# Background blocks one unit sooner, behind the second score of an even unit, with their rows added between two maxima steps

## The chip, the cores and the metric

The kernel runs on one core of a Trainium2 chip. The metric is the device time of one execution in microseconds. Five engines work side by side: TensorE (PE; its weight loads are shown as PEld), VectorE (DVE), ScalarE (ACT), GpSimd (POOL) and SyncE (SP), which here only issues transfers. Each takes its instructions from a queue of its own, and they wait for one another by semaphores.

## What is computed

A transformer layer with the norm behind each part, in float32: two sequences of 1024 rows with 512 features, grouped attention (32 query heads of 16, 8 key heads) with rotary angles, then a gated feed-forward part with 1408 inner features.

```python
Q, K = rope(x @ Wq.T + bq), rope(x @ Wk.T + bk)          # 32 and 8 heads of 16
V = x @ Wv.T + bv
w = softmax(einsum('bhqd,bhkd->bhqk', Q, repeat(K, 4)) / sqrt(16))
x = layernorm(x + (w @ repeat(V, 4)) @ Wo.T + bo)
g, u = (x @ gate_w.T) * gate_s, (x @ up_w.T) * up_s
x = layernorm(x + ((silu(g) * u) @ down_w.T) * down_s)
```

## The kernel before

**Units.** Attention is cut into 256 units: 16 pairs n of sequence and key head, with 16 units v each (two halves of the queries by 8 tiles of 128 keys). Code writes a unit as u = 16 n + v, or as the pair (n, v). PE does in each unit, by the loop that begins at L704: four scores (`scores`, L470, 512 queries by 128 keys for one query head g), each followed by one half step of maxima (`advance`, `maxima_half`, L448), and once the weighted sum of the unit before (`weigh`, L489): behind the last score in an even unit, behind the third in an odd one. A score tile stands in one of three PSUM banks, used in turn; the fourth score of an odd unit takes two of them, 128 columns and 384. ACT turns each into exponents (`exponent`, L784), which frees the bank.

**Maxima.** Softmax needs the largest score of each row before the scores are built. So PE computes the products of queries and keys twice: `maxima_half` runs 24 steps (12 units) ahead. A step has two halves, 512 keys each, in one of two slots of two banks. DVE reduces a step either whole (L991) or by halves (L987), alternately (`maximum`). A slot, or half slot, is free for PE once DVE has read it. When 16 steps are done, which is in units with u % 8 == 3, DVE joins the results (L1005). POOL splits them into a high and a low part in the same unit (`split_max`, L1316 and L1318). DVE transposes the parts behind its first step of the next unit (`turn_max`, L1021), and SP writes them to memory and reads them back into extra rows of the queries (`write_max`, L1564 and L1567) in units with u % 8 == 4. The scores of unit u % 8 == 0 that comes four units later need them.

**Background.** Eleven blocks of other work are set between the scores. Six project queries or keys for later (`project_at`: (n, v) to a job; 24 products of 512 columns, L387), one builds the values of the second sequence (`values_at`, products of 128 columns, L429), four make the attention's output rows (`out_at`, 24 products, L515). They stand in odd units, v = 3 or 11, behind the third score and ahead of the weighted sum. A block borrows two of the three score banks (`free_banks`), one half of the work in each.

A projected half is taken out by ACT (`evacuate_raw`, L770). Then SP swaps the halves of the rows by two transfers (`swap_halves`, L1530 and L1531), and POOL turns them by the angles in three passes over 1024 columns (`rope`, L1329, L1330, L1332). In later units ACT rounds each half and POOL takes the remainder (`low_half`, L1337), then SP writes both out; these steps are placed by `rope_end`. Values and output rows are added by DVE (`add_values`, L970; `add_rows`, L1057), and in the units of `norm_at` DVE also does the norm of the rows of the block before (`first_norm`, L1033 to L1041).

**Order.** All queues are written out by hand: each engine's program is one loop over the units with tests on (n, v). The order inside one unit of POOL's loop is, cut to three of its steps (L1464 to L1476):

```python
if u % 8 == 3 and apart(steps_done(u) // 16 - 1):
    split_max(steps_done(u) // 16 - 1)
if at_u in project_at:
    rope(project_at[at_u])
...
    elif what in ("h0", "h1"):
        low_half(j, int(what == "h1"))
```

Of the kernel before, what the change touches and what calls it, by code (L numbers as in the profile page):

```python
# [70 lines left out]
def post_ln_layer(nc, xT_d, x_d, wqk_d, wv_d, bqk_d, bv_d, wo_d, bo_d, wf_d, gs_d, us_d, ds_d,  # L71
# [6 lines left out]
    with ExitStack() as ctx:  # L78
# [123 lines left out]
        def bank(i):  # L202
            return PS2[:, i, :] if i < 3 else PV[:, :]
# [57 lines left out]
        stream = [(n, qt, g) for n in range(NG) for qh in range(2) for qt in range(4 * qh, 4 * qh + 4)  # L261
                  for g in (2, 0, 3, 1)]
        jobs = [(0, 1), (0, 2), (0, 3), (1, 4), (1, 0), (1, 1), (1, 2), (1, 3)]
        project_at = {(1, 11): 2, (4, 11): 3, (5, 3): 4, (6, 3): 5, (8, 3): 6, (8, 11): 7}
        rope_end = {(0, 1): (0, "h0"), (0, 2): (0, "h1"), (0, 3): (0, "out"),
                    (0, 4): (1, "rope"), (0, 8): (1, "h0"), (0, 10): (1, "h1"), (0, 11): (1, "out")}
        for at_u, j in project_at.items():
            u0 = 16 * at_u[0] + at_u[1] + 7
            rope_end.update({divmod(u0, 16): (j, "h0"), divmod(u0 + 2, 16): (j, "h1"), divmod(u0 + 3, 16): (j, "out")})
        values_at = (2, 11)  # L270
        out_at = {(10, 3): 0, (10, 11): 1, (11, 3): 2, (11, 11): 3}
        norm_at = {(10, 11): 0, (11, 3): 1, (11, 11): 2}
        recip_at = {(2, 13): 0, (4, 13): 1, (6, 5): 2, (8, 5): 3, (10, 5): 4, (12, 5): 5, (14, 5): 6}
        divide_at = {divmod(16 * n + v + 4, 16): kc for (n, v), kc in recip_at.items()}
        gather_at = {(n, {0: 13}.get(n, 5)): n + 2 for n in range(NG - 2)}
# [31 lines left out]
        score_bank = {}  # L307
# [13 lines left out]
            return c if p == len(pieces(c)) - 1 else (c, p)  # L321

        def free_banks(u):
            last = score_bank[4 * u + 2, 0]
            return (last + 1) % 3, last

        def ffn_slots(x):
# [34 lines left out]
        def tensor(e):  # L362
# [94 lines left out]
            def scores(u, g, p=0):  # L457
                n, v = divmod(u, 16)
                qh, kt = divmod(v, 8)
                c = 4 * u + g  # L460
                cols, i = pieces(c)[p], score_bank[c, p]
                clear(bank_free[i])
                w.wait_ge(*max_in[n % 3].at(2 * n + qh))
                if n == 0:
                    for point in first_rows[qh]:
                        w.wait_ge(*point)
                else:
                    w.wait_ge(*rows_in[n % 3].at(n))
                rows = slice(64 * (g // 2), 64 * (g // 2) + NC_ + 2)
                e.matmul(score_tile(i)[:, cols], Kt[n % 3][rows, 128 * kt:128 * kt + 128],  # L470
                         Qt[n % 3][rows, g % 2, 512 * qh + cols.start:512 * qh + cols.stop], start=True, stop=True).then_inc(
                    *pe_score.next(piece(c, p)))
                bank_free[i] = act_exp.at(piece(c, p))
# [216 lines left out]
            def background(u):  # L690
                at_u, pair = divmod(u, 16), free_banks(u)
                if at_u in project_at:
                    for h, i in enumerate(pair):
                        project_half(project_at[at_u], h, i, (0, 1, 2, 3))
                if at_u == values_at:
                    for t in range(8):
                        value_rows(1, t, pair[t // 4])
                if at_u in out_at:
                    t2 = out_at[at_u]
                    out_project(False, 0, t2, [bank(i) for i in pair], [bank_free[i] for i in pair])  # L700
                    for j, i in enumerate(pair):
                        bank_free[i] = dve_y.at((False, 0, 2 * t2 + j))

            for u in range(SPLIT):  # L704
                at_u = divmod(u, 16)
                for g in range(4):
                    scores(u, g)
                    advance(1)
                    if len(pieces(4 * u + g)) == 2:
                        scores(u, g, 1)  # L710
                    if u >= 1 and g == (3, 2)[u % 2]:
                        background(u)
                        weigh(u - 1)
                if at_u == (15, 1):
                    flag_sum()
                if at_u == (15, 2):
                    w.wait_ge(*dve_flag.at("flag"))
# [12 lines left out]
        def scalar(e):  # L730
# [188 lines left out]
            for u in range(SPLIT):  # L919
                at_u = divmod(u, 16)  # L920
                for g in range(4):
                    exponent(u, g)
                    if g == 2 and at_u in project_at:
                        for h, i in enumerate(free_banks(u)):
                            evacuate_raw(project_at[at_u], h, i)
                if u >= 1:
                    finish(u - 1)
                if at_u in rope_end and rope_end[at_u][1] in ("h0", "h1"):
                    round_half(rope_end[at_u][0], int(rope_end[at_u][1] == "h1"))
                if at_u == (15, 2):  # L930
                    w.wait_ge(*dve_flag.at("flag"))
# [11 lines left out]
        def vector(e):  # L943
# [22 lines left out]
            def add_values(b, h, i):  # L966
                w.wait_ge(*pe_val.at((b, h)))
                w.wait_ge(*landed["bv"].at())
                w.wait_ge(*pool_one.at())
                e.tensor_tensor(  # L970
                    Vp[:, b, 4 * h:4 * h + 4, :, 0:HD], bank(i).rearrange("p (t v c) -> p t v c", t=4, v=NKV),
                    bv[:, :].rearrange("p (o v c) -> p o v c", o=1, v=NKV).to_broadcast([128, 4, NKV, HD]),
                    ALU.add).then_inc(*dve_val.next((b, h)))

            def maximum(k, halves=(0, 1)):
                if k >= len(stream):
                    return
                s, hh = slot_of(k), k // 16
                g, qt = stream[k][2], stream[k][1]
                c0 = 4 * g + qt % 4  # L980
                if hh >= 2:
                    w.wait_ge(*low_max(hh - 2))
                if by_halves(k):
                    for h in halves:
                        w.wait_ge(*pe_max.at((k, 0) if h == 0 else k))
                        col = nmx[:, hh % 2, c0 + 16 * (h == 0):c0 + 16 * (h == 0) + 1]
                        e.tensor_reduce(col, slot_pair(s)[:, h, :], AX.X, ALU.max, negate=True).then_inc(  # L987
                            *dve_max[s].next((k, 0) if h == 0 else k))
                else:
                    w.wait_ge(*pe_max.at(k))  # L990
                    e.tensor_reduce(nmx[:, hh % 2, c0:c0 + 1], slot_pair(s), AX.XY, ALU.max, negate=True).then_inc(  # L991
                        *dve_max[s].next(k))
                if 1 in halves and k % 16 == 15:
                    join_max(hh)
                    if not apart(hh):
                        split_max(hh)
                        turn_max(hh)
                if k % 16 == 0 and k > 16 and apart(hh - 1):
                    turn_max(hh - 1)
# [48 lines left out]
            def first_norm(x, b, t2):  # L1048
                key = (x and b == 1, b, t2)
                measure_rows(rows_of(b, t2), [dve_y.at((x and b == 1, b, 2 * t2 + 1))], key)  # L1050
                scale_rows(rows_of(b, t2), key, dve_x1, key)
# [201 lines left out]
            for u in range(SPLIT):  # L1253
                at_u = divmod(u, 16)
                maximum(next(steps))
                k = next(steps)
                if at_u in norm_at or at_u in out_at or at_u == values_at:
                    maximum(k, (0,))
                    if at_u in norm_at:
                        first_norm(False, 0, norm_at[at_u])  # L1260
                    if at_u == values_at:
                        for h, i in enumerate(free_banks(u)):
                            add_values(1, h, i)
                    if at_u in out_at:
                        add_rows(False, 0, out_at[at_u], [bank(i) for i in free_banks(u)])
                    maximum(k, (1,))
                else:
                    maximum(k)
                if at_u in recip_at:
                    reciprocal(recip_at[at_u])  # L1270
                if at_u == (15, 0):
                    w.wait_ge(*pool_low.at((FI - 1, 2)))
                    e.tensor_reduce(lowb[:, :], lowsum, AX.X, ALU.max).then_inc(*dve_flag.next("max"))
                if at_u == (15, 1):
                    w.wait_ge(*pe_flag.at())
                    e.tensor_scalar(flag[0:1, 0:1], slot_pair(before_flag % 2)[0:1, 0, 0:1], 0.0, None,
                                    ALU.is_gt).then_inc(*dve_flag.next("flag"))
                if at_u == (15, 2):
                    w.wait_ge(*dve_flag.at("flag"))
# [559 lines left out]
```

## Time and profile before

| | us |
|---|---|
| median of 3 runs (lowest, highest) | 1038.73 (1037.86, 1039.15) |
| profiled execution | 1039.11 |
| its span, first to last instruction | 1037.2 |
| PE busy | 1017.1 |
| DVE busy | 794.2 |
| ACT busy | 664.9 |
| POOL busy | 278.6 |

The profiled execution lies 0.4 us above the median, and 1.9 us of it lie around the span. Busy times are shares of the whole span, of which attention takes about the first 755 us and the feed-forward part the rest; the change lies in attention alone. Busy PE time includes matmuls that overlap, so the share says that PE is hardly ever empty, not how fast it goes; that is read from the distance between like instructions.

### The profile page before, as it was taken

The numbers are of one execution on the slowest core, as the hardware profiler recorded it, in microseconds if no ns is written. First come the engines' busy times: TensorE is split into PE (matmuls) and PEld (weight loads), VectorE is DVE, ScalarE is ACT, GpSimd is POOL, SyncE is SP. The second block draws the span as 40 slices with busy tenths as digits, with TensorE's granted clock in tenths as the row PEclk, the third lists the DMA queues.
The fourth block names the chain that finished last, engine by engine and source line by source line (L and its number), as shares of the span: only waits on it lengthen the run. The fifth ranks groups of instructions, "written<-read, shape, count | busy, mean of one in ns | idle before, by whom it ended". The sixth has DMA issues, their size and how long they took to land.

```text
span 1037.2 us, 15698 instructions
## 1 busy us (share of the span) xinstructions
PE 1017.1 (98%) x5858; PEld 534.6 (52%) x5858; DVE 794.2 (77%) x1139; ACT 664.9 (64%) x1346; POOL 278.6 (27%) x287
## 2 busy tenths in 40 slices
PE   8999999999999999999999999999999999999996
PEld 3643344433444433443444433333348888888885
DVE  5899978899779799779898898899822566563535
ACT  2359977789778898779666687888872420222221
POOL 2742021152245532246310055444101001000002
PEclk9999999999999999999999999899999999999999
DMA  5273517233215522345140447431238311311011
GB/s 205 82 211 105 123 34 215 59 99 87 54 53 143 91 73 48 85 85 133 35 79 12 119 136 151 109 128 41 100 119 195 120 41 41 82 51 32 1 40 43
DMA packets 64433, 94.88 MB, mean 91 GB/s; under 512 B 37536, under 2 KB 37920, under 8 KB 62272
## 3 DMA queue, kind: packets, MB, share of 16 engines
q1 hardware_dynamic: 63776, 93.10, 34.4%
q8 instruction: 48, 0.79, 0.3%
q10 hardware_dynamic: 576, 0.72, 0.2%
q14 instruction: 33, 0.27, 0.1%
HBM read 53.95 MB, written 27.00 MB: 78 GB/s over the span
## 4 chain that ended last, share of the span: by engine, by line
PE 94%; DVE 3%; ACT 1%; DMA 1%; issue 0%; POOL 0%; SPq 0%; POOLq 0%; DVEq 0%
PE PS L470 29%; PE PV L489 24%; PE PSA L559 15%; PE PS L576 6%; PE PSA L448 5%; PE PS L387 4%; PE PS L515 2%; PE PSA L515 2%; PE PV L576 2%; PE PSA L387 1%; PE PS L429 1%; ACT Bn L784 1%; DVE nmx L991 1%; DVE nmx L987 1%; DMA mscr<-mrow 1%; DMA A<-in_wqk 0%
## 5 line engine op out<-in xcount | busy, mean ns | idle before, releaser
L784 ACT ACTIVATE Bn<-PS 128x512 f32<-128x512 f32 x1128 | 535.5, 559 | 97.9 <-PE PS L470 85.6
L448 PE MATMUL PSA<-Kt,Qt 48*128 48x512 f32 x1024 | 388.5, 461 | 1.2 <-DVE Kt L964 0.8
L470 PE MATMUL PS<-Qt,Kt 50*128 50x512 f32 x1128 | 385.8, 436 | 3.8 <-DMA Qt<-mscr 2.5
L987 DVE TENSOR_REDUCE nmx<-PSA 128x1 f32<-128x512 f32 x512 | 327.3, 679 | 39.7 <-PE PSA L448 39.7
L470 PEld LDWEIGHTS PS<-Qt,Kt 50*128 50x128 f32 x1128 | 183.4, 185 | 311.5 <-ACT Bn L784 284.3
L991 DVE TENSOR_REDUCE nmx<-PSA 128x1 f32<-128x1024 f32 x256 | 312.2, 1219 | 22.6 <-PE PSA L448 20.3
L489 PE MATMUL PV<-Bn 128*32 128x512 f32 x2048 | 274.6, 608 | 0.0
L448 PEld LDWEIGHTS PSA<-Kt,Qt 48*128 48x128 f32 x1024 | 176.3, 184 | 11.7 <-DVE nmx L987 3.3
L559 PE MATMUL PSA<-x1Th,wr 128*128 128x512 f32 x344 | 135.5, 394 | 0.0
L559 PE MATMUL PSA<-x1Tl,wr 128*128 128x512 f32 x344 | 134.5, 391 | 0.0
L820 ACT ACTIVATE sg<-PSA,gs 128x512 f32<-128x512 f32 x43 | 29.6, 690 | 128.1 <-PE PSA L559 128.1
L1089 DVE SCALAR_TENSOR_TENSOR sg<-PSA,us,sg 128x512 f32<-128x512 f32 x43 | 32.2, 749 | 93.1 <-ACT sg L820 93.1
L489 PEld LDWEIGHTS PV<-Bn 128*32 128x32 f32 x2048 | 40.6, 108 | 76.0 <-issue 65.3
L1316 POOL CAST msp<-nmx 128x16 fp32r<-128x16 f32 x30 | 5.9, 196 | 262.3 <-DVE nmx L1005 262.3
L559 PEld LDWEIGHTS PSA<-x1Th,wr 128*128 128x128 f32 x344 | 64.6, 188 | 17.9 <-issue 3.6
L559 PEld LDWEIGHTS PSA<-x1Tl,wr 128*128 128x128 f32 x344 | 64.7, 188 | 13.3
L1402 POOL TENSOR_SCALAR ve<-mv 128x2 f32<-128x2 f32 (+1 forms) x11 | 2.8, 258 | 247.1 <-DVE mv L1036 247.1
L833 ACT CAST hTh<-sg 128x512 fp32r<-128x512 f32 x38 | 23.6, 620 | 44.0 <-DVE sg L1089 36.8
L1109 DVE TENSOR_TENSOR hTl<-sg,hTh 128x512 fp32r<-128x512 f32 x38 | 26.3, 692 | 33.1 <-ACT hTh L833 33.0
L1381 POOL TENSOR_TENSOR Bn<-Bn 128x1024 f32<-128x1024 f32 x8 | 19.4, 2419 | 98.4 <-DMA Bn<-rscr 98.4
L576 PE MATMUL PS<-wr,hTh 128*128 128x512 f32 x114 | 44.7, 392 | 0.0
L576 PE MATMUL PS<-wr,hTl 128*128 128x512 f32 x114 | 44.5, 391 | 0.0
(170 smaller groups left out, 909.4 us busy)
## 6 DMA issues: line engine op xcount, KB each, us to landing
Qt<-pscr SPq DMA_DIRECT2D x90, 128.0 KB, 5.2
A<-in_wf SPq DMA_DIRECT2D x11, 768.0 KB, 7.1
wr<-A SPq DMA_DIRECT2D x33, 256.0 KB, 2.8
pscr<-A SPq DMA_DIRECT2D x16, 512.0 KB, 3.5
vscr<-Bn SPq DMA_DIRECT2D x32, 256.0 KB, 3.0
Kt<-pscr SPq DMA_DIRECT2D x90, 64.0 KB, 2.8
A<-A SPq DMA_DIRECT2D x16, 256.0 KB, 3.7
Bn<-vscr SPq DMA_DIRECT2D x8, 512.0 KB
```

Source lines behind the costliest of these rows:

```text
L387: op = e.matmul(ps, v, t, start=first and i == 0, stop=last and end)
L448: op = e.matmul(PSA[:, 2 * s + h, :], Qt[n % 3][p:p + NC_, g % 2, 128 * qt:128 * qt + 128], Kt[n % 3][p:p + NC_, 512 * h:512 * h + 512], s ...
L470: e.matmul(score_tile(i)[:, cols], Kt[n % 3][rows, 128 * kt:128 * kt + 128], Qt[n % 3][rows, g % 2, 512 * qh + cols.start:512 * qh + cols. ...
L489: op = e.matmul(PV[32 * g:32 * g + 32, :], Bn[:, o:o + 32], Pb[c % NP_], start=(kt == 0), stop=(kt == 7), tile_position=(0, 32 * g))
L515: op = e.matmul(ps, t_, v, start=(k == 0 and i == 0), stop=(k == KT - 1 and i == len(pairs) - 1))
L559: op = e.matmul(gate_bank(x, q, j), v, t, start=(k == 0 and m == 0), stop=(k == KT - 1 and m == (1 if x else 0)))
L576: op = e.matmul(bank(t), v, t_, start=(i == 0 and m == 0), stop=(i == FI - 1 and end))
L784: e.activation(Pb[c % NP_][:, cols], score_tile(score_bank[c, p])[:, cols], ACT.Exp, scale=0.25).then_inc(*act_exp.next(piece(c, p)))
L820: e.activation(sg[q % 2], gate_bank(x, q, 0), ACT.Silu, scale=gs[:, i:i + 1]).then_inc(*act_silu.next((x, q)))
L987: e.tensor_reduce(col, slot_pair(s)[:, h, :], AX.X, ALU.max, negate=True).then_inc(*dve_max[s].next((k, 0) if h == 0 else k))
L991: e.tensor_reduce(nmx[:, hh % 2, c0:c0 + 1], slot_pair(s), AX.XY, ALU.max, negate=True).then_inc(*dve_max[s].next(k))
L1089: e.scalar_tensor_tensor(out=out, in0=gate_bank(x, q, 1), scalar=us[:, i:i + 1], in1=sg[q % 2], op0=ALU.mult, op1=ALU.mult).then_inc(*dve_ ...
```

## The change

All eleven blocks stand one unit sooner (v = 2 or 10) and, inside the unit, behind the second score and its half step instead of behind the third. The banks they borrow are those that are free there. ACT takes the projected halves out behind the second exponent. DVE adds rows and values (and does the norm) between the unit's whole step and the one by halves, which is no longer split around them. The swap on SP and the rope on POOL, which go by the same dictionary, move one unit with the block; the steps of `rope_end` stay in their units. The number of instructions stays the same.

```diff
-        project_at = {(1, 11): 2, (4, 11): 3, (5, 3): 4, (6, 3): 5, (8, 3): 6, (8, 11): 7}
+        project_at = {(1, 10): 2, (4, 10): 3, (5, 2): 4, (6, 2): 5, (8, 2): 6, (8, 10): 7}
...
-            u0 = 16 * at_u[0] + at_u[1] + 7
+            u0 = 16 * at_u[0] + at_u[1] + 8
...
-        values_at = (2, 11)
-        out_at = {(10, 3): 0, (10, 11): 1, (11, 3): 2, (11, 11): 3}
-        norm_at = {(10, 11): 0, (11, 3): 1, (11, 11): 2}
+        values_at = (2, 10)
+        out_at = {(10, 2): 0, (10, 10): 1, (11, 2): 2, (11, 10): 3}
+        norm_at = {(10, 10): 0, (11, 2): 1, (11, 10): 2}
...
         def free_banks(u):
-            last = score_bank[4 * u + 2, 0]
+            last = score_bank[4 * u + 1, 0]
...
+                    if g == 1:
+                        background(u)
                     if u >= 1 and g == (3, 2)[u % 2]:
-                        background(u)
                         weigh(u - 1)
...
-                    if g == 2 and at_u in project_at:
+                    if g == 1 and at_u in project_at:
                         for h, i in enumerate(free_banks(u)):
                             evacuate_raw(project_at[at_u], h, i)
...
-                if at_u in norm_at or at_u in out_at or at_u == values_at:
-                    maximum(k, (0,))
-                    if at_u in norm_at:
-                        first_norm(False, 0, norm_at[at_u])
...
-                    maximum(k, (1,))
-                else:
-                    maximum(k)
+                if at_u in norm_at:
+                    first_norm(False, 0, norm_at[at_u])
...
+                maximum(k)
```

## Rows read from the trace of the kernel before

**Rows 1.** The page's table of engines: busy us, share of the span, instructions.

```profile
PE 1017.1 (98%) x5858; PEld 534.6 (52%) x5858; DVE 794.2 (77%) x1139; ACT 664.9 (64%) x1346; POOL 278.6 (27%) x287
```

**Rows 2.** Busy time of each engine in a quiet stretch; waits there (us, times, longest).

```profile
460.00:500.00 40.00, 40.00 (x272) 15.17 (x270) 38.86 (x54) 36.15 (x77) 26.50 (x23) 1.00 0.36 98
PEld PS L470 <- ACT Bn L784: 20.1, 40, 0.8
```

**Rows 3.** PE's timeline over two units: start, duration, engine, line, operation, tiles, shape, count.

```profile
475.88 1.07 PE L489 MATMUL PV<-Bn 128*32 128x512 f32 x8
...
478.00 0.49 PE L470 MATMUL PS<-Qt,Kt 50*128 50x512 f32 x1
...
478.92 1.07 PE L489 MATMUL PV<-Bn 128*32 128x512 f32 x8
...
480.48 0.39 PE L470 MATMUL PS<-Qt,Kt 50*128 50x512 f32 x1
...
480.81 1.07 PE L489 MATMUL PV<-Bn 128*32 128x512 f32 x8
```

**Rows 4.** PE's timeline around the projection in unit (8,3): first and last product, sums.

```profile
417.63 1.07 PE L489 MATMUL PV<-Bn 128*32 128x512 f32 x8
...
419.80 0.50 PE L387 MATMUL PS<-xh,wh 128*128 128x512 f32 x1 [0.22 <-ACT Bn L784]
...
425.16 0.39 PE L387 MATMUL PS<-xl,wh 128*128 128x512 f32 x1
425.48 1.07 PE L489 MATMUL PV<-Bn 128*32 128x512 f32 x8
```

**Rows 5.** ACT, DVE, POOL, SP behind that block; POOL's group of `low_half`, mean in ns.

```profile
425.59 0.69 ACT L770 ACTIVATE A<-PS,bqk 128x512 f32<-128x512 f32 x1 [2.04 <-PE PS L387]
...
429.03 0.20 DVE L1021 STREAM_TRANSPOSE mrow<-msp 128x32 f32<-128x32 f32 x1
429.16 1.24 DVE L987 TENSOR_REDUCE nmx<-PSA 128x1 f32<-128x512 f32 x2
...
428.05 0.20 POOL L1316 CAST msp<-nmx 128x16 fp32r<-128x16 f32 x1 [25.14 <-DVE nmx L1005]
428.32 0.22 POOL L1318 TENSOR_TENSOR msp<-nmx,msp 128x16 fp32r<-128x16 f32 x1
430.67 2.38 POOL L1329 TENSOR_TENSOR A<-A 128x1024 f32<-128x1024 f32 x1 [2.13 <-DMA A<-A]
...
435.46 2.39 POOL L1332 TENSOR_TENSOR A<-A 128x1024 f32<-128x1024 f32 x1
...
429.26 0.59 SPq L1564 DMA_DIRECT2D mscr<-mrow  x1
431.27 0.53 SPq L1567 DMA_DIRECT2D Qt<-mscr  x2
...
L1337 POOL TENSOR_TENSOR A<-A 128x512 f32<-128x512 f32 x16 | 20.5, 1283 | 34.3 <-ACT A L776 34.3
```

**Rows 6.** DVE's timeline in unit (10,11), a block with rows and norm.

```profile
537.85 1.28 DVE L1033 BATCH_NORM_STATS2 st<-x1a 128x6 f32<-128x512 f32 x2
...
541.50 0.68 DVE L1057 TENSOR_TENSOR x1a<-x1a,PS 128x512 f32<-128x512 f32 x1
```

**Rows 7.** SP and PE around 645 us; then busy times, clock (1.00 is full) and DMA.

```profile
637.27 0.56 SPq L1564 DMA_DIRECT2D mscr<-mrow  x1
645.38 0.56 SPq L1567 DMA_DIRECT2D Qt<-mscr  x2
...
643.25 1.07 PE L489 MATMUL PV<-Bn 128*32 128x512 f32 x8
...
647.33 0.47 PE L470 MATMUL PS<-Qt,Kt 50*128 50x512 f32 x1 [2.53 <-DMA Qt<-mscr]
...
656.79 0.64 PE L489 MATMUL PV<-Bn 128*32 128x512 f32 x4
...
648.20:655.00 6.80, 6.61 (x29) 2.01 (x29) 4.14 (x5) 3.87 (x8) 1.56 (x2) 0.50 0.52 166
```

More of the change, by code:

```diff
@@ L1256, in vector @@
                 k = next(steps)
-                if at_u in norm_at or at_u in out_at or at_u == values_at:
-                    maximum(k, (0,))
-                    if at_u in norm_at:
-                        first_norm(False, 0, norm_at[at_u])
[L1261 to L1265, printed above, removed]
-                    maximum(k, (1,))
-                else:
-                    maximum(k)
+                if at_u in norm_at:
+                    first_norm(False, 0, norm_at[at_u])
+                if at_u == values_at:
+                    for h, i in enumerate(free_banks(u)):
+                        add_values(1, h, i)
+                if at_u in out_at:
+                    add_rows(False, 0, out_at[at_u], [bank(i) for i in free_banks(u)])
+                maximum(k)
                 if at_u in recip_at:
```

## Prediction

> **What bounds the kernel now.** The table of engines comes first: TensorE (PE) is busy for 98% of the span, so the page names it as the bound [rows 1]. That figure counts overlapping, modelled matmul ends, so I went on to one quiet stretch. There VectorE (DVE) is busy 38.86 of 40 us and ScalarE (ACT) 36.15, and PE's weight loads for scores waited on ACT's exponents for 20.1 us [rows 2]. Three engines run in lockstep, and none has much slack. The third view, PE's timeline of two units, shows the beat. The weighted sums (L489) start at 475.88 in an odd unit, 478.92 in the even one, 480.81 in the next odd one [rows 3]: 3.04 us and 1.89 us, 4.93 for a pair. The reader should see why 3.04 is so long: the third score of the even unit starts at 478.00, 0.92 before the sum, whereas in the following unit the third score (480.48) stands 0.33 before its sum. The stretch up to 478.00 and behind it is paced by exponents.
>
> The fourth view is a block of background work as it lies now, in an odd unit [rows 4]. From the sum at 417.63 to the sum at 425.48 are 7.85 us where 1.89 would stand without the block, so it costs 5.96. Its 24 products start from 419.80 to 425.16; the first waited 0.22 us for an exponent. During it ACT and DVE run dry, and right behind it comes the weighted sum (0.99 us), in which ACT has nothing either.
>
> The fifth view is what the other engines do after this block [rows 5]. Call T the start of its last product (425.16). ACT empties the second bank from 425.59 to 426.28 (T+1.12). GpSimd (POOL) splits the finished maxima at 428.05 and 428.32, ready at 428.54 (0.49 in all). Only then does it start the rope, at 430.67 (T+5.51), released by the swap transfer, and ends it at 435.46 + 2.39 = 437.85 (T+12.7).
>
> **The change, part by part.**
>
> *The block's place.* Now PE goes from the second score of the even unit to the block, then to the third and fourth score, then to the sum. The first bank that the block takes is the one that the third score waited for, so it starts where that score starts now, 478.00 - 475.88 = 2.12 behind the odd sum [rows 3]. Then 5.36 for the products [rows 4], 0.32 to the next score (as 425.16 to 425.48), and 0.33 + 0.33 for two scores that no exponent holds up, since ACT has drained meanwhile. That gives 8.46 for what is 3.04 without the block: 5.42 instead of 5.96, a gain of 0.54; with 0.23 between the two scores it would be 0.64. I take 0.56. The 11 blocks (six projections, one of values, four of output rows) give 11 x 0.56 = 6.2 us. ACT's evacuation ends at T+1.12 and the next score that needs the bank comes behind the sum at T+1.97; this cover is 0.8 us thick.
>
> *VectorE.* The rows are added after the whole step and before both halves, instead of between the halves. In the three units that also normalise, statistics and scaling take 541.50 - 537.85 = 3.65 us [rows 6]. They begin 0.6 sooner than now and still end inside the 5.4 us of products, so the first row is added before PE wants the bank. Both halves come some 0.6 us later; the slot they hold is wanted at T+2.5 and the first of them is read by about T+1.7. I cost this at nothing. Were the cover gone, it would be one 0.68 us reduction in each of 5 blocks.
>
> *What moves with the six projections.* The same dictionary places the swap on SP's queue and the rope on POOL's. On SP nothing is passed: the maxima are written in the next but one unit, still behind the swap. On POOL two queued instructions are passed: the split of the maxima is issued in units with u % 8 == 3, before the rope in the same unit today. With the rope in u % 8 == 2 it stands ahead of that split. The split then waits for the rope, the rope for the swap, and the swap for the evacuation.
>
> Who waits for the split: DVE's transpose of the maxima, queued behind its first reduction of unit u % 8 == 4, and behind it every later reduction. The times follow from T. PE: sums at T+0.98 (even), +2.87 (odd), +5.91 (even), and the third product of maxima in the unit after would start at 2.87 + 3.04 + 1.56 = T+7.47. DVE would come to its transpose at about T+6.5. But POOL ends the rope at T+12.7, the split takes 0.49 more [rows 5], so T+13.2; transpose 0.13 to the next reduction, that one 0.68 to its end, and PE may refill the half slot at T+14.1. Stall of PE: 14.1 - 7.47 = 6.6 us. PE's lead of two slots is already in the 7.47. Six of them: 39.6 us. DVE works off its two waiting steps while PE restarts; I take 0 for it, at most 0.3 each.
>
> *Two collisions.* Units (5,2) and (8,10) are also those in which POOL rounds the first half of the job before (L1337, 1.28 us [rows 5]). It was ahead of the rope by one unit and now falls between rope and split: 2 x 1.3 = 2.7 us with its gap.
>
> *The clock.* PE stands idle for 6.3 us in each stall. The trace has one such case: a wait of 2.53 us before 647.33, and from 648.2 to 655.0 the granted clock is 0.50, which is 1.2 instead of 2.4 GHz [rows 7]. From the sum at 643.25 to the one at 656.79 are 13.54 us against 3.04 + 1.89 + 3.04 = 7.97, a loss of 5.6; the wait put off the first score by 2.7, so the slow clock cost 2.8. With longer idle I take the same 2.8 for each of the six, 16.8 us. It is bounded below by 0 (the clock stays up) and above by 4.2, half again as much, if the clock takes longer to come back.
>
> The Trainium skill, "TensorE: Matmul & The Clock Gate", Part 1, says that the array runs at 1.2 GHz by default when idle and is let up to 2.4 GHz by sustained work. The trace agrees, with the 0.50 behind 2.53 us of waiting. By that rule all six stalls end at the low clock; without it the sum is 16.8 us shorter.
>
> **Sum**, against the profiled execution (1039.1 us, of it 1037.2 span): -6.2 + 39.6 + 2.7 + 16.8 = +52.9, so 1092.0. The median of the runs shown is 0.4 lower, so 1091.6.
>
> **Rivals.**
>
> (1) *Stalls without the slow clock.* The trace shows one fall of the clock in the middle of the span, so one case carries the whole term. If a stall of this kind does not bring it on, 1091.6 - 16.8 = 1074.8.
>
> (2) *The maxima come too late for the scores as well.* Behind the transpose (T+13.3) SP writes the maxima, 2.0 us to the reads (429.26 to 431.27), and a read landed 1.95 us after its issue (645.38 [rows 7] to the score at 647.33). That is T+17.8 with the gaps; the first score that needs them comes at about T+20.7. So 2.9 us remain. Where weights were being loaded, the write took 645.38 - 637.27 = 8.1 us [rows 7]; 6.1 - 2.9 = 3.2 us more in each of six, 1091.6 + 19 = 1111. Against it: the weights are loaded only from unit (11,5) on.
>
> (3) *The other side: the split is not held by the rope.* If POOL could take the split, whose maxima are ready, ahead of the rope, or if swap and rope were done by T+6.0 rather than T+12.7, DVE would find the split ready at T+6.5. No stall then, no slow clock, and only the gain remains: 1038.7 - 6.2 = 1032.5. The point that decides is whether the split's low part is ready at T+6.5. Against it: the rope's three passes alone take 7.2 us from a start at T+5.5, and nothing in the change touches POOL's order.
>
> The Trainium skill, "PSUM — Partial Sum Buffer", section "Engine vs sequencer instructions", calls the queues of ScalarE, VectorE and GpSimdE "strict FIFO". By it rival 3 is out; no row here shows POOL passing anything, and none could show that it never does.
>
> **Chances.** Forecast 0.72 (1080 to 1101: six times the clock's 0.8 to 4.2 around it); rival 1 0.10; rival 2 or otherwise longer 0.10; rival 3 0.05; stalls much smaller than worked out 0.03, of which 0.02 within 0.2%. A measurement of this kernel can tell about 0.2% from no change. Faster 0.05, same 0.02, slower 0.93. The range takes in rival 1 and the upper bound of the clock: 1073 to 1103.
>
> **What the changed profile would show.** The block's price: sum to sum 8.4 to 8.5 us in ten blocks, followed by 1.89. The chain of steps: on POOL the split directly behind the rope's third pass, or behind L1337, and in the table of waits DVE's transpose waiting six times for the split, 5 to 7 us each. PE's loads for L448 then wait for DVE's half reduction for about as long. The granted clock falls to 0.50 six times in the first half of the span. The four blocks of output rows and the one of values show no stall, only 0.5 to 0.6 us less. I am wrong in the main if the transpose does not wait; wrong in size if rope or swap take another time, or the clock stays at 1.00.

## The result and the profile after

The changed kernel takes 1094.0 us in the median of 4 runs (1092.2 to 1096.6) against 1038.3 for the kernel before: a ratio of 1.0535, 95% interval 1.0518 to 1.0551. The profiled execution took 1096.6 us with a span of 1094.7, so it lies 2.6 above the median. Lines of code after the change are some numbers off those of before: the transpose is L1022, the half reductions L988, the split L1313 and L1315, the rope L1326, L1327 and L1329.

The page's table of engines, after, answers to [rows 1]: PE's busy time rose by 19 us and the others' hardly at all, so 39 of the 57.5 us by which the span grew are idle PE.

```profile
PE 1035.7 (95%) x5858; PEld 540.9 (49%) x5858; DVE 795.7 (73%) x1139; ACT 665.4 (61%) x1346; POOL 278.0 (25%) x287
```

The tables of waits of DVE and of PE, after (who <- for whom: us in total, times, longest). Neither line exists in the kernel before.

```profile
DVE mrow L1022 <- POOL msp L1315: 41.3, 6, 7.7
PE PSA L448 <- DVE nmx L988: 38.7, 6, 7.2
```

Six waits of the transpose for the split, six waits of PE for the half reduction behind it. Four times the transpose waited 6.5 us, twice 7.7. The first of them, in the timelines of PE, POOL and DVE behind the projection in (1,10), whose last product starts at 134.5:

```profile
137.43 1.06 PE L489 MATMUL PV<-Bn 128*32 128x512 f32 x8
...
140.47 1.07 PE L489 MATMUL PV<-Bn 128*32 128x512 f32 x8
...
142.04 0.39 PE L470 MATMUL PS<-Qt,Kt 50*128 50x512 f32 x1
148.47 0.79 PE L448 MATMUL PSA<-Kt,Qt 48*128 48x512 f32 x1 [6.04 <-DVE nmx L988]
149.19 1.93 PE L489 MATMUL PV<-Bn 128*32 128x512 f32 x8
...
140.05 2.39 POOL L1326 TENSOR_TENSOR A<-A 128x1024 f32<-128x1024 f32 x1 [24.74 <-DMA A<-A]
142.39 2.35 POOL L1327 TENSOR_TENSOR A<-A 128x1024 f32<-128x1024 f32 x1
144.82 2.34 POOL L1329 TENSOR_TENSOR A<-A 128x1024 f32<-128x1024 f32 x1
147.10 0.20 POOL L1313 CAST msp<-nmx 128x16 fp32r<-128x16 f32 x1
147.38 0.22 POOL L1315 TENSOR_TENSOR msp<-nmx,msp 128x16 fp32r<-128x16 f32 x1
...
139.94 1.22 DVE L992 TENSOR_REDUCE nmx<-PSA 128x1 f32<-128x1024 f32 x1
147.63 0.21 DVE L1022 STREAM_TRANSPOSE mrow<-msp 128x32 f32<-128x32 f32 x1 [6.47 <-POOL msp L1315]
147.77 1.25 DVE L988 TENSOR_REDUCE nmx<-PSA 128x1 f32<-128x512 f32 x2
```

Read it from the bottom up. DVE ends its first reduction of unit (1,12) at 141.1 and could transpose; the maxima were joined at 140.0. POOL takes the split only at 147.10, behind three passes that began at 140.05. PE's third score of the next unit starts at 142.04, and the half step of maxima that belongs to it at 148.47. Compare [rows 5], where the split stood 2.1 us ahead of the rope.

The third view is busy time and granted clock of three stretches there (us; busy PE, PEld, DVE, ACT, POOL with counts; clock; DMA share; GB/s):

```profile
142.40:148.50 6.10, 0.06 (x2) 0.03 (x1) 0.87 (x3) 1.17 (x3) 5.04 (x5) 0.69 0.00 0
148.50:155.00 6.50, 6.50 (x28) 2.24 (x28) 5.09 (x7) 2.74 (x6) 0.00 (x0) 0.50 0.04 9
155.00:160.00 5.00, 5.00 (x37) 1.81 (x33) 4.14 (x6) 3.99 (x9) 0.00 (x0) 1.00 0.00 0
```

While PE idles the clock falls to its lower level (0.50, 1.2 GHz) and stays there for 6.5 us of resumed work; the weighted sum takes 1.93 us instead of 1.07, as behind the wait of [rows 7].

**Where 57.5 us of span come from.** I compared the starts of like weighted sums in both traces. The start of a weighted sum is a good mark, since every unit has one. Nine of the eleven blocks became 0.45 to 0.56 us cheaper, together -4.8. The block in (6,2) became 0.4 dearer, that in (10,10) 2.7 with the unit behind it. The six stalls add 6.8 or 6.9 (four) and 8.0 (two), together 43.4. The four units behind each add 2.1 to 3.5, together 15.4. One microsecond is from the start of the program, ahead of any changed instruction, and about 0.6 is given back in small amounts.

Block (10,10) is the one thing of a new kind. POOL, DVE and PE there:

```profile
592.17 2.41 POOL L1378 TENSOR_TENSOR Bn<-Bn 128x1024 f32<-128x1024 f32 x1 [16.16 <-DMA Bn<-rscr]
594.55 0.24 POOL L1399 TENSOR_SCALAR ve<-mv 128x2 f32<-128x2 f32 x1
594.87 0.73 POOL L1401 TENSOR_TENSOR ve<-ve,half 128x2 f32<-128x2 f32 x1
595.63 1.00 DVE L1042 TENSOR_SCALAR x1a<-x1a,mv,ve 128x512 f32<-128x512 f32 x2 [2.96 <-POOL ve L1401]
596.55 1.28 DVE L1058 TENSOR_TENSOR x1a<-x1a,PS 128x512 f32<-128x512 f32 x2
597.29 0.50 PE L470 MATMUL PS<-Qt,Kt 50*128 50x512 f32 x1 [1.62 <-DVE x1a L1058]
```

A division (L1378) stands in unit (10,9) and now runs when the norm needs its spread (L1399 and L1401), which waits behind it. The norm ends late, the rows are added late, and the third score waits 1.62 us for its bank. The clock fell behind that wait too, for 3.4 us. In (6,2) PE's first product waited 0.9 us for a split of weights that POOL does behind ten microseconds of bias additions; the split ended at 361.05 and the product began at 361.20.

### The profile page after: what moved, and what is told of

Read it like the earlier page. It is cut to its first block, busy times and chain, and to the rows that moved or that the text cites. A ratio compares the mean times of both kernels' runs of the same rounds, so it can differ in the third digit from the quotient of the medians.

```text
span 1094.7 us, 15698 instructions
## 1 busy us (share of the span) xinstructions
PE 1035.7 (95%) x5858; PEld 540.9 (49%) x5858; DVE 795.7 (73%) x1139; ACT 665.4 (61%) x1346; POOL 278.0 (25%) x287
## 4 chain that ended last, share of the span: by engine, by line
PE 85%; POOL 5%; DMA 3%; DVE 3%; issue 2%; ACT 1%; SPq 0%; POOLq 0%; DVEq 0%
PE PS L470 24%; PE PV L489 21%; PE PSA L559 15%; PE PSA L448 6%; PE PS L576 6%; PE PS L387 4%; PE PSA L515 2%; DMA A<-A 2%; PE PV L576 2%; PE PS L515 2%; PE PSA L387 1%; POOL A L1326 1%; PE PS L429 1%; POOL A L1329 1%; POOL A L1327 1%
## 5 line engine op out<-in xcount | busy, mean ns | idle before, releaser
L448 PE MATMUL PSA<-Kt,Qt 48*128 48x512 f32 x1024 | 395.7, 472 | 40.0 <-DVE nmx L988 38.7
L988 DVE TENSOR_REDUCE nmx<-PSA 128x1 f32<-128x512 f32 x512 | 327.4, 679 | 38.8 <-PE PSA L448 38.8
L470 PEld LDWEIGHTS PS<-Qt,Kt 50*128 50x128 f32 x1128 | 186.7, 189 | 319.7 <-ACT Bn L785 273.0
L489 PE MATMUL PV<-Bn 128*32 128x512 f32 x2048 | 284.8, 629 | 0.0
L448 PEld LDWEIGHTS PSA<-Kt,Qt 48*128 48x128 f32 x1024 | 180.2, 189 | 52.9 <-DVE nmx L988 44.6
L1399 POOL TENSOR_SCALAR ve<-mv 128x2 f32<-128x2 f32 (+1 forms) x11 | 2.9, 260 | 238.5 <-DVE mv L1037 238.5
L1378 POOL TENSOR_TENSOR Bn<-Bn 128x1024 f32<-128x1024 f32 x8 | 19.4, 2427 | 128.4 <-DMA Bn<-rscr 128.4
L1313 POOL CAST msp<-nmx 128x16 fp32r<-128x16 f32 x30 | 5.9, 198 | 173.9 <-DVE nmx L1006 173.8
L1326 POOL TENSOR_TENSOR A<-A 128x1024 f32<-128x1024 f32 x8 | 19.1, 2385 | 111.9 <-DMA A<-A 111.2
```

Of the source, the lines that this page charges most:

```text
L448: op = e.matmul(PSA[:, 2 * s + h, :], Qt[n % 3][p:p + NC_, g % 2, 128 * qt:128 * qt + 128], Kt[n % 3][p:p + NC_, 512 * h:512 * h + 512], s ...
L489: op = e.matmul(PV[32 * g:32 * g + 32, :], Bn[:, o:o + 32], Pb[c % NP_], start=(kt == 0), stop=(kt == 7), tile_position=(0, 32 * g))
L1326: e.tensor_tensor(raw, raw, cosT, ALU.mult).then_inc(*pool_rope.next((j, "cos")))
```

## The experiments

**e1_rope_behind_split: POOL's rope alone put back.** Every block stays in its new place.

```diff
-                if at_u in project_at:
-                    rope(project_at[at_u])
+                if divmod(u - 1, 16) in project_at:
+                    rope(project_at[divmod(u - 1, 16)])
```

> The changed kernel with the rope of the six projections put back one unit on GpSimd alone, behind the split of the maxima; all blocks stay where the change put them. Theory (rope ahead of the split in GpSimd's queue): no wait of VectorE's transpose for the split, no fall of the clock behind it, so only the gain of place remains, about 0.53 us in each of 11 blocks, less what two single waits take (0.9 us in unit (6,2), 2.7 us in unit (10,10)): 1033 to 1036 us. Rival A (the loss comes from the block's new place, such as both half reductions coming later): 1085 us or more. Rival B (place gives nothing by itself): 1038 to 1039 us.

Measured: 1035.6 us against 1038.8, ratio 0.9964 (0.9951 to 0.9978). POOL's timeline has the split ahead again, and no wait of the transpose is left:

```profile
139.19 0.20 POOL L1313 CAST msp<-nmx 128x16 fp32r<-128x16 f32 x1 [24.77 <-DVE nmx L1006]
139.47 0.22 POOL L1315 TENSOR_TENSOR msp<-nmx,msp 128x16 fp32r<-128x16 f32 x1
139.65 2.39 POOL L1326 TENSOR_TENSOR A<-A 128x1024 f32<-128x1024 f32 x1
```

So the whole loss came with one call in POOL's queue, and the place of the blocks is a small gain. By the starts of the sums it is 0.44 to 0.59 us in nine blocks less 0.3 in (6,2) and 0.2 in (10,10), 4.2 us in all. The block in (10,10) has the same order as in the changed kernel, with the division ahead of the spread, but it cost much less here: the division began 1.4 us behind the block's first product instead of 2.3, PE waited less, and the clock stayed up.

```profile
PE PS L470 <- DVE x1a L1058: 0.7, 1, 0.7
```

So what that order costs hangs on when the division's data land. About 1.3 of the gain was lost again in this execution at the wait for the maxima that stands in [rows 7], which took 4.2 us here instead of 2.5.

**e2_before_rope_first: the same exchange in the kernel before.**

```diff
+                if at_u in project_at:
+                    rope(project_at[at_u])
                 if u % 8 == 3 and apart(steps_done(u) // 16 - 1):
                     split_max(steps_done(u) // 16 - 1)
-                if at_u in project_at:
-                    rope(project_at[at_u])
```

> The kernel before with one edit: in the units of the projections GpSimd does the rope ahead of the split of the maxima instead of behind it. Theory: the same stall, and a longer one, since the block stands one unit nearer to the transpose: PE's next half slot is wanted at T+4.9 instead of T+7.5 and comes free at about T+14.3, so 9.4 us and 2.5 us of slow clock in each of six, 71 us: about 1110 us. Rival A (the loss belongs to the new place): 1038 to 1040 us.

Measured: 1108.1 us, ratio 1.0676 (1.0652 to 1.0699). Each of the six stalls adds 9.34 to 9.42 us, where 9.4 was worked out. PE's table of waits:

```profile
PE PSA L448 <- DVE nmx L987: 51.4, 6, 8.6
```

This is the cleanest sign of the cause: nothing else moved, and the stall is longer by about the time that the block stands nearer to the transpose (2.5 us, where 2.6 was worked out).

**e3_two_passes: a shorter rope.** One of its three passes, the multiplication by the sines, is left out for the six projections, so the kernel computes something else; only its time is of use.

```diff
-                e.tensor_tensor(qrot, qrot, sinT, ALU.mult).then_inc(*pool_rope.next((j, "sin")))
-                w.wait_ge(*pool_rope.at((j, "sin")))
+                if j < 2:
+                    e.tensor_tensor(qrot, qrot, sinT, ALU.mult).then_inc(*pool_rope.next((j, "sin")))
+                w.wait_ge(*pool_rope.at((j, "sin" if j < 2 else "cos")))
```

> The changed kernel with the rope of the six projections cut from three passes over 1024 columns to two (the multiplication by the sines is left out, so part of the computation is missing). Theory: each stall becomes shorter by just one pass, 2.4 us, 14.3 us in all, and the clock still falls behind 3.7 us of idleness: 1079 to 1081 us. Rival C (VectorE waits for something else, the swap's transfer or the read-back of the maxima): 1092 to 1095 us.

Measured: 1079.1 us, ratio 1.0383 (1.0367 to 1.0400), 14.9 less than the changed kernel. The transpose's six waits, now 5.4 us at most:

```profile
DVE mrow L1022 <- POOL msp L1315: 27.5, 6, 5.4
```

41.3 - 27.5 = 13.8 us, 2.3 for each pass of 2.35 us left out. The rope's length goes into the stall one for one. The clock still fell behind the 3.7 us of idleness left in four of the stalls and the 4.9 in the two others.

**e4_filler: PE kept at work in the stall.** Products with zero weights (`zero`, set once at the start; `FILL` is 6) are added to the weighted sum's bank, so the sum is the same.

```diff
...
                     scores(u, g)
+                    if g == 2 and divmod(u - 3, 16) in project_at:
+                        w.wait_ge(*dve_const.at())
+                        for _ in range(FILL + (at_u in ((5, 5), (8, 13)))):
+                            e.matmul(PV[:, :], zero[:, :], Bn[:, vo:vo + 512], start=False, stop=False)
                     advance(1)
...
```

> The changed kernel with PE kept at work during each of the six stalls: six (seven in units (5,5) and (8,13)) products of zero weights, 0.86 us each, added to the weighted sum's bank, behind the third score and ahead of the half step of maxima that has to wait. Theory (idleness brings the clock down, which costs 2.1 to 3.5 us behind each stall): the granted clock stays at 1.00 there, the stalls keep their end, and about 15 us come back: 1077 to 1081 us. Rival D (the 2.1 to 3.5 us are VectorE and ScalarE catching up, not the clock): 1093 to 1096 us.

Measured: 1083.5 us, ratio 1.0434 (1.0418 to 1.0450), so 10.5 less than the changed kernel where 15 was expected; between the two profiled executions it is 13.8 of span. The transposes' waits stayed (42.4 us). Behind the first stall the clock stays up:

```profile
148.30:155.00 6.70, 6.70 (x46) 2.52 (x47) 6.63 (x9) 4.25 (x9) 0.00 (x0) 1.00 0.03 6
```

The four units behind each stall add -0.01 to 0.12 us in five cases instead of 2.1 to 3.5. In the sixth, behind block (5,2), the swap's transfer landed 1.0 us later than in the changed kernel and the rope with it, so the filler ran out early: PE idled 2.04 us ahead of 320.30, the clock was at 0.50 from 322.3 to 325.7, and 1.1 us were lost. The slow clock is the cause of what is lost behind the stalls. That cost differs between executions: behind the six stalls it was 15.4 us in the changed kernel, 13.8 in e6 and 12.9 in e5. That may be part of the 4 us between the changed kernel's runs, which was not measured. Why the medians differ by less than the profiled executions is not settled beyond that.

**e5_low_half_first: the two collisions.**

```diff
+                if at_u in project_at and at_u in rope_end:
+                    low_half(rope_end[at_u][0], 0)
                 if at_u in project_at:
                     rope(project_at[at_u])
...
-                    elif what in ("h0", "h1"):
+                    elif what in ("h0", "h1") and at_u not in project_at:
```

> The changed kernel with GpSimd's remainder of the first half (low_half) put ahead of the rope in units (5,2) and (8,10). Theory (what stands between rope and split lengthens the stall by its own length): the two long waits of the transpose shrink from about 8.0 to 6.85 us like the other four, since the remainder is done while GpSimd waits for the swap anyway; 2.3 us less in all, about 1092 us. Rival (these two stalls are longer for another reason, such as transfers): they stay at 8.0 us.

Measured: 1090.5 us, ratio 1.0502 (1.0485 to 1.0519). All six waits are now 6.46 to 6.49 us:

```profile
DVE mrow L1022 <- POOL msp L1315: 38.9, 6, 6.5
```

41.3 - 38.9 = 2.4 us, 1.2 for each; the rest of the 3.5 was not traced to anything.

**e6_divide_later: the norm in (10,10).**

```diff
+        divide_at[10, 11] = divide_at.pop((10, 9))
```

> The changed kernel with one division (L1378, 2.4 us) moved from unit (10,9) to unit (10,11) on GpSimd, so that it no longer stands ahead of the spread that VectorE's norm in block (10,10) waits for. Theory (norm late by that division, rows added late, score bank late): PE's 1.6 us gap before the third score of (10,10) and the fall of the clock behind it vanish, the sum-to-sum distance of that block falls from 9.1 to the 7.4 of the other blocks of rows, 2 to 3 us less in all, about 1091.5 us. Rival (the norm does not fit into the block's products once the rows are added ahead of both halves): the gap stays above 1 us.

Measured: 1091.5 us, ratio 1.0509 (1.0492 to 1.0526). PE's gap in (10,10) is gone, and so is the fall of the clock behind it; the block and the unit behind it lie 3.2 us lower by the starts of the sums. The spread now comes at once and no longer follows the division:

```profile
590.60 0.24 POOL L1400 TENSOR_SCALAR ve<-mv 128x2 f32<-128x2 f32 x1 [16.79 <-DVE mv L1038]
590.92 0.73 POOL L1402 TENSOR_TENSOR ve<-ve,half 128x2 f32<-128x2 f32 x1
...
599.11 2.39 POOL L1379 TENSOR_TENSOR Bn<-Bn 128x1024 f32<-128x1024 f32 x1
```

**e7_split_on_vector: the split taken from POOL's queue instead of the rope.** In the six half heads DVE splits the maxima itself.

```diff
+        own_split = [(16 * n + v + 1) // 8 + 1 for n, v in project_at]
         def apart(hh):
-            return 1 <= hh < 2 * NG - 1
+            return 1 <= hh < 2 * NG - 1 and hh not in own_split
```

> The changed kernel, GpSimd's rope still in the block's own unit, but in the six half heads concerned VectorE splits the maxima itself, as it does for the first and the last. Theory (only the split's place in GpSimd's queue links the rope to the scores): no stall and no slow clock, at a price of two short VectorE instructions in six units: 1034 to 1038 us. Rival (rope, swap or late read-back of the maxima hold PE up in another way as well): above 1050 us.

Measured: 1068.8 us, ratio 1.0278 (1.0258 to 1.0298). My theory was wrong here by more than 30 us, and the rival right: something else holds PE up. POOL, DVE and PE behind the first block:

```profile
139.73 2.36 POOL L1328 TENSOR_TENSOR A<-A 128x1024 f32<-128x1024 f32 x1 [24.73 <-DMA A<-A]
139.74 2.39 DVE L1015 CAST msp<-nmx 128x16 fp32r<-128x16 f32 x1
142.06 2.33 POOL L1329 TENSOR_TENSOR A<-A 128x1024 f32<-128x1024 f32 x1
142.16 2.27 DVE L1017 TENSOR_TENSOR msp<-nmx,msp 128x16 fp32r<-128x16 f32 x1
144.46 0.21 DVE L1024 STREAM_TRANSPOSE mrow<-msp 128x32 f32<-128x32 f32 x1
...
145.84 0.79 PE L450 MATMUL PSA<-Kt,Qt 48*128 48x512 f32 x1 [4.19 <-DVE nmx L994]
```

No semaphore is missing: DVE runs the two instructions of 16 columns, and each lasts until the POOL pass under way ends, 2.39 and 2.27 us where the same forms take 0.17. In three of the six units only the second waited. There the first had begun 0.01 to 0.02 us ahead of the pass, while in the other three it began as little behind it:

```profile
279.04 0.17 DVE L1015 CAST msp<-nmx 128x16 fp32r<-128x16 f32 x1
279.06 2.38 POOL L1328 TENSOR_TENSOR A<-A 128x1024 f32<-128x1024 f32 x1 [19.68 <-DMA A<-A]
```

PE idled 4.2 us where both waited and 1.9 where one did, and the clock fell behind five of the six.

**e9_vector_split_quarters: e7 with shorter POOL instructions.**

```diff
+                parts = [slice(256 * i, 256 * i + 256) for i in range(4)] if j >= 2 else [slice(0, 1024)]
-                e.tensor_tensor(raw, raw, cosT, ALU.mult).then_inc(*pool_rope.next((j, "cos")))
+                for c in parts:
+                    e.tensor_tensor(raw[:, c], raw[:, c], cosT[:, c], ALU.mult).then_inc(*pool_rope.next((j, "cos")))
...
```

> The kernel of e7 (VectorE splits the maxima itself in six half heads) with each pass of the six ropes cut on GpSimd into four instructions of 256 columns. In e7 VectorE's two instructions of 16 columns, 0.17 us elsewhere, took 2.2 to 2.4 us and ended together with a GpSimd pass over 1024 columns. Theory (two VectorE instructions whose operands lie in SBUF wait for the GpSimd instruction under way, to its end): with pieces of about 0.6 us each takes at most some 0.8 us, PE's gaps of 1.9 to 4.2 us shrink below 1 us, the clock stays up: 1036 to 1043 us. Rival (VectorE waits for the whole rope or for semaphores, whatever the length of a piece): as e7, 1065 to 1072 us.

Measured: 1040.8 us, ratio 1.0022 (1.0013 to 1.0032). DVE's second instruction, first in e7, then here (ns, least/median/most of 8):

```profile
L1017 DVE TENSOR_TENSOR msp<-nmx,msp x8: 174/2230/2266, 52.6 to 774.7; 128x16 fp32r<-128x16 f32 x8
```

```profile
L1017 DVE TENSOR_TENSOR msp<-nmx,msp x8: 174/590/655, 51.2 to 741.2; 128x16 fp32r<-128x16 f32 x8
```

The wait follows the length of the single POOL instruction, 2.35 us or 0.7. PE's waits for the half reduction sum to 2.1 us instead of 18.4, and the clock no longer falls behind them. That settles e7.

**e10_quarters: the control.** The same pieces in the changed kernel, split still on POOL.

> The changed kernel with each pass of the six ropes cut into four instructions of 256 columns, the split of the maxima still on GpSimd behind them: the control to e9. Theory (the queue's order alone makes the stall): the transpose still waits for the whole rope, which becomes a little longer by its nine further instructions: 1093 to 1098 us. Rival (it is the length of single GpSimd instructions that holds VectorE up in the changed kernel too): below 1080 us.

Measured: 1100.1 us, ratio 1.0587 (1.0569 to 1.0604), 2 us above what I gave. The pieces are less efficient than I took them for: three passes last 8.5 us instead of 7.1, and the waits grow from 41.3 to 49.2.

```profile
DVE mrow L1022 <- POOL msp L1315: 49.2, 6, 9.0
```

So in the changed kernel it is the order of the queue that counts, and the length of the single instruction only adds.

**e8_mended: what the runs point to.** e1 with three edits more.

```diff
+        divide_at[10, 11] = divide_at.pop((10, 9))
+        ffn_at[12, 13] = ffn_at.pop((12, 8)) + ffn_at[12, 13]
...
-                if at_u == (5, 12):
+                if at_u == (5, 13):
                     add_bo(0, u)
```

> The kernel of e1 with three further edits: the first addition of the output bias one unit later, behind the split of the weights that the block in (6,2) waits for; the division moved to (10,11) as in e6; one 768 KB weight load moved from unit (12,8) to (12,13), behind the write of the maxima that waits among such loads. Theory: the single gaps of 0.85 and 0.7 us go, and the gap of 4.2 us with its fall of the clock becomes shorter or goes, 2 to 5 us less than e1: 1030 to 1034 us. Rival: the gap before unit (13,0) comes from the reads of the keys and queries alone and stays; 1034 to 1036 us.

Measured: 1030.1 us, ratio 0.9921 (0.9906 to 0.9936), the fastest of all. All eleven blocks now gain 0.44 to 0.55 us, and the clock falls nowhere but at the end.

```profile
core 0: 1026.2 us, clock 0.998
```

**e11_before_load_later: how much of it is the block's place.** The weight load's edit alone, in the kernel before.

> The kernel before with the last edit of e8 alone: one 768 KB weight load moved from unit (12,8) to (12,13), behind the write of the maxima. In the trace of before, PE waited 2.53 us for the read-back and then ran 6.8 us at the low clock, 5.6 us in all. Theory (the write stands behind that load's packets, and the wait brings the clock down): the wait falls below 1 us, the clock stays at 1.00, 4 to 6 us less: 1033 to 1035 us, and the place of the blocks then accounts for about 4 to 5 us of the gain of e8. Rival (the packets of keys and queries ahead of it are what delays the write): within 1 us of before.

Measured: 1034.1 us, ratio 0.9963 (0.9951 to 0.9976). PE's wait for the read-back fell to 1.2 us, where I had said below 1, and the clock stayed at 1.00 from 640 to 660:

```profile
PE PS L471 <- DMA Qt<-mscr: 1.2, 1, 1.2
...
640.00:660.00 20.00, 18.58 (x128) 7.21 (x131) 18.23 (x27) 16.50 (x36) 10.66 (x15) 1.00 0.48 167
```

The write of the maxima was still slow: from its issue to the read-back's were 6.6 us instead of 8.1, against 2.0 in [rows 5]. So that load makes up a quarter of the delay, and the rival, which blamed the keys and queries, may be right about the rest; no run moved those. The wait shortened by 1.3 us, and most of the 4.1 us came from the clock that no longer fell.

So 4.1 of e8's 8.5 us go with that load, which has nothing to do with the change, and that leaves 4.4 for the place of the blocks with POOL's queue set right around it. By the starts of the sums in e8's profile the eleven blocks gain 5.8 us, and in that execution the wait for the read-back is gone altogether, so the split of the 8.5 is good to about a microsecond.

## Why the prediction held, point by point

The forecast was 1091.6 us; 1094.0 was measured, 2.4 above it. The mechanism was the forecast one: rope ahead of split, transpose behind both, PE behind the transpose, and a slow clock behind each stall.

- *The stall.* 6.6 us each were worked out, 6.85 measured in four of six. POOL ended the rope at T+12.6 and PE resumed at T+13.9 in the first block, as forecast; what is above 6.6 stands in the restart, since with the clock held up (e4) the same stall added 6.53 to 6.57 in four of six. (The terms as written in the prediction add up to T+14.0 and 6.5 us, 0.1 less than it says.) e2 confirmed the same sum for another place of the block (9.4 and 9.3 to 9.4), and e3 that the rope's length enters it fully.
- *The collisions.* 1.3 us each forecast, 1.2 measured (e5).
- *The clock.* 2.8 us each forecast from one row, 2.1 to 3.5 measured, 15.4 instead of 16.8; that one row gave the right size is partly luck, as the cost scatters by more than a microsecond. The mechanism was shown by e4. The fall began during the idle time: of the 10.2 us at the low clock behind the first stall, only 6.5 were work.
- *The place.* 0.56 us a block forecast, 0.53 measured in nine blocks (nine in e1 too, all eleven in e8). The sum-to-sum distance was 8.46 to 8.58 us in eight of them, where 8.4 to 8.5 was given, and 10.2 in the block of values, whose products are of another size.
- *Where it was wrong: "I cost this at nothing".* The step on VectorE's norm, that it would "still end inside the 5.4 us of products", failed in one block. I checked that 3.65 us of norm fit into the products, but took that length from a unit in which POOL was free. With the blocks one unit sooner, POOL's division comes ahead of the spread; that cost 2.7 us here, and 3.2 us went with it in e6 (in e1 the same order cost 0.8, the lost gain included). The step said "On POOL two queued instructions are passed", and there was a third relation to check: those that the moved work now runs into. The same holds for the 0.9 us in (6,2). Two signs named ahead were off with it or beside it: the clock fell a seventh time, in (10,10), and two of the transpose's six waits were 7.7 us, above the "5 to 7".
- *Rival 2* (maxima late for the scores) did not come about: no wait for the read-back appeared but that of the kernel before, 2.5 us. *Rival 1* (no slow clock) is out by all six falls. *Rival 3* is out too: POOL took the split behind the rope six times out of six, and e1, in which the order alone differs, came out within 3.1 us of where rival 3 had put its time, 1032.5 forecast and 1035.6 measured.

That the total came out within 2.4 us is in part luck. Profile against profile the span grew by 57.5 us where 52.9 was forecast: the stalls were 1.1 us longer (43.4 against 42.3), the clock cost 1.4 less, the eleven blocks together gained 1.7 instead of 6.2, and 0.4 came from elsewhere. The profiled execution is also the slowest of the four, 2.6 above their median, and so half of the miss does not show in the medians.

## What to carry to other kernels

When a table of positions drives several engines' programs, moving an entry moves a step in each queue: list for every queue what the step is now ahead of, and who waits for that. A long instruction on a side engine cost nothing here until something short and urgent stood behind it in the queue, or, as e7 showed, ran on VectorE beside it; one call put on the wrong side of a 0.5 us split turned a gain of 0.4% into a loss of 5%. And count a stall of the matrix engine with its echo, since in this kernel a quarter of the loss came after the stalls, at the low clock.

## What the runs showed of the hardware

**Small VectorE work waits for a whole GpSimd instruction.** In e7 a copy of 16 columns (one operand in SBUF) and a subtraction of 16 columns (two operands in SBUF) lasted 2.39 and 2.27 us beside GpSimd passes over 1024 columns, and 0.17 us otherwise. The copy waited in the three units where it began 0.01 to 0.02 us behind the pass, and took 0.17 us in the three where it began as little ahead of it. With GpSimd pieces of 0.7 us the subtraction lasted 0.59 (e9). The transpose (0.20 to 0.21 us) and the reductions out of PSUM (1.2 us) beside the same passes kept their lengths. The Trainium skill, "SBUF — State Buffer", section "SBUF: two separate sides", says that VectorE and GpSimd share a pair of ports as an exclusive lock, held for a full instruction, for VectorE instructions with two SBUF inputs or in a two-port mode; the trace agrees, with 2.27 us for the subtraction. The copy has one SBUF input and waited as well, so here it falls under the page's second condition or outside its rule; no run tells which.

**The clock fell behind short waits too.** A gap of 1.62 us in the changed kernel, in a stretch that was otherwise busy, was followed by 3.4 us at 0.50, and so were gaps of 1.87 and 2.04 us in e4 and of 2.05 in e9. Gaps of 1.9 us in e7 were followed by a fall twice and once not. A gap of 1.51 us in e5, the same wait in (10,10), was not, nor were those of 0.7 to 1.24 us in the other runs. Behind the six long stalls the low level lasted 10.2 us (five) or 13.7 us (one), of which the time after PE had resumed was 6.5 us in the first.

**Filler work left its neighbours nearly alone.** Six or seven products of zero weights in each stall, 0.86 us each, changed the other engines' work in the stalls little (the transposes' waits sum to 42.4 us instead of 41.3, of which 1.0 lies in the one late transfer), and the median fell by 10.5 us.
